# Attention: where ScalarE reads a side product, at the head of the next slot or between that slot's two exponentials

## The reference

```python
q, k, v = x @ Wq + bq, x @ Wk + bk, x @ Wv + bv      # 16 heads of 8
attn = q @ k.T / sqrt(8) + alibi                      # 1024 x 1024 for each head
attn = where(causal, attn, min); p = softmax(attn)
out = (p @ v) @ Wo + bo
x = layernorm(x + out); logits = x @ router_w.T + router_bias
```

## Time and profile before

| what | value |
|---|---|
| median of three runs | 1295.51 us |
| the profiled execution | 1296.66 us, of which the span is 1294.9 us |
| granted clock of TensorE, mean over the span | 0.87 |
| busy over the span | PE 972.5 us (75%), DVE 795.9 us (61%), ACT 549.7 us (42%), POOL 489.5 us (38%) |
| attention of layer 1, its slots | from about 349 to 957 us |
| ScalarE's exponentials (L2143) | 384, 299.1 us in all |
| VectorE's maxima (L2205) | 640, 374.6 us in all |

### The profile page before, as it was taken

How to read it: one execution, slowest core, us unless ns; L and a number is a source line. 1 busy time by engine, 2 the same in 40 slices (tenths; PEclk the granted TensorE clock), 3 DMA queues, 4 the chain that set the end, 5 groups by cost and what they waited for, 6 DMA issues and landing times. The chain is left out here.

```text
span 1294.9 us, 20993 instructions
## 1 busy us (share of the span) xinstructions
PE 972.5 (75%) x7024; PEld 549.3 (42%) x7024; DVE 795.9 (61%) x2147; ACT 549.7 (42%) x878; POOL 489.5 (38%) x484
## 2 busy tenths in 40 slices
PE   5772118962477799788987888788778989998892
PEld 4662016741222233232322333233237877885451
DVE  3757860022585789577884779778927542554664
ACT  1331004422134667566564666465564433431142
POOL 4001044525603700153002541043544544556775
PEclk8985558985569999898988999799999998999996
DMA  4224103421310301121010312225127755652122
GB/s 114 66 66 157 26 10 91 119 63 34 97 51 16 94 28 36 29 81 41 27 46 15 93 53 63 81 67 198 49 65 207 212 168 153 177 137 64 46 68 73
DMA packets 113439, 106.19 MB, mean 82 GB/s; under 512 B 17770, under 2 KB 95210, under 8 KB 112696
## 3 DMA queue, kind: packets, MB, share of 16 engines
q1 hardware_dynamic: 74216, 65.53, 16.8%
q0 software_dynamic: 12048, 25.71, 7.3%
q10 hardware_dynamic: 27072, 13.64, 3.7%
HBM read 59.60 MB, written 41.94 MB: 78 GB/s over the span
## 5 line engine op out<-in xcount | busy, mean ns | idle before, releaser
L2205 DVE TENSOR_REDUCE maxima<-psum 128x1 f32<-128x512 f32 (+3 forms) x640 | 374.6, 625 | 107.6 <-PE psum L2018 106.5
L2143 ACT ACTIVATE probs<-psum 128x1024 f32<-128x1024 f32 (+3 forms) x384 | 299.1, 809 | 266.6 <-PE psum L2038 264.4
L2018 PE MATMUL psum<-ka,qa 61*128 61x512 bf16 (+3 forms) x768 | 205.2, 358 | 30.8 <-ACT side_xT L1386 8.8
L2053 PE MATMUL psum<-probs,v_wide 128*32 128x512 f32 (+3 forms) x1536 | 178.0, 538 | 0.6 <-ACT outT L2115 0.4
L2038 PE MATMUL psum<-qa,ka 64*128 64x512 bf16 (+3 forms) x768 | 170.6, 341 | 1.5 <-ACT probs L2143 1.4
L1530 POOL DMA_INDIRECT sorted<-x_rows,to_row x76 | 76.3, 1003 | 209.2 <-ACT probs L2143 118.0
L2016 PE MATMUL psum<-mask 64*128 64x128 bf16 x512 | 98.1, 236 | 52.7 <-DVE maxima L2205 10.7
L2560 ACT ACTIVATE g_silu<-psum 128x512 f32<-128x512 f32 x80 | 47.8, 597 | 179.2 <-PE psum L2466 106.9
L1456 POOL DMA_INDIRECT w_gu<-expert_out,to_row x64 | 66.0, 1031 | 143.5 <-ACT probs L2143 100.9
L2018 PEld LDWEIGHTS psum<-ka,qa 61*128 61x128 bf16 x768 | 62.2, 98 | 113.2 <-DVE maxima L2205 67.5
L2016 PEld LDWEIGHTS psum<-mask 64*128 64x128 bf16 x512 | 42.2, 98 | 160.2 <-DVE maxima L2205 86.1
(11 more groups left out here) (326 smaller groups left out, 1614.4 us busy)
## 6 DMA issues: line engine op xcount, KB each, us to landing
g_rows<-sorted SPq DMA_DIRECT2D x192, 64.0 KB
expert_out<-g_y ACTq DMA_DIRECT2D x48, 256.0 KB, 2.7
w<-in_W SPq DMA_DIRECT2D x16, 256.0 KB, 3.0
w_gu<-in_gu SPq DMA_DIRECT2D x4, 1024.0 KB, 10.8
sorted<-blank SPq DMA_DIRECT2D x54, 64.0 KB
q_steps<-w_gu SPq DMA_DIRECT2D x12, 256.0 KB
k_steps<-w_gu SPq DMA_DIRECT2D x12, 256.0 KB
qa<-q_steps SPq DMA_DIRECT2D x30, 96.0 KB
```

Source lines behind the costliest of these rows:

```text
L2018: mm = pe.matmul(bank[:, h * width:(h + 1) * width], qa[b][at:at + ROWS_MAX, (h0 + h) % PER_SIDE, qt * P:(qt + 1) * P], ka[b][at:at + ROWS ...
L2053: mm = pe.matmul(B[OUT][32 * h:32 * (h + 1), q0 - c * HALF:HALF], v_wide[s.buf][:, j, h, PAD * (1 - c):PAD * (1 - c) + 32], probs[k % PRIN ...
L2143: act.activation(probs[k % PRING][:, 2 * pair:2 * pair + 2, 0:w], PS[:, 2 * pair:2 * pair + 2, 0:w], ACT.Exp).then_inc(exps, 1)
L2205: dve.tensor_reduce(maxima[:, seg, h0:h0 + heads, qt], bank[:, 0:heads * width].rearrange("p (h k) -> p h k", h=heads), AX.X, ALU.max).the ...
```

## The change

The call of `emit_side_scalar` leaves `beside(g)`, where it stood behind the first exponential of the slot, and is made at the head of the slot, ahead of the wait for the probability buffer and ahead of the first exponential. The rest of `beside` stays where it is. Nothing is added or removed; the order of instructions on the other engines is the same.

```diff
                 def beside(g):
                     b, r = divmod(g, BATCH_SLOTS)
-                    if g - 1 in SIDE_AT and SIDE_AT[g - 1][0] in ("turn_x", "q", "k", "turn_att", "turn_new"):
-                        emit_side_scalar(act, S, Q, SIDE_AT[g - 1])
                     if b + 1 < BATCH and SCALE_AT <= r < SCALE_AT + 4:
...
                         w = (c + 1) * HALF - q0
+                        g = s.n * SLOTS + k
+                        if g - 1 in SIDE_AT and SIDE_AT[g - 1][0] in ("turn_x", "q", "k", "turn_att", "turn_new"):
+                            emit_side_scalar(act, S, Q, SIDE_AT[g - 1])
                         if k >= PRING or not flags[0]:
                             act.wait_ge(pv, s.n * SLOTS + k - PRING + 1)
```

## The result

The changed kernel takes 1256.98 us (median of four runs, 1253.79 to 1259.1), the kernel before beside it 1291.38. The ratio is 0.972, with a 95% interval from 0.965 to 0.979. Timed a second time, six runs of it beside eleven of the kernel before, it took 1251.46 us against 1290.29: 0.968, from 0.963 to 0.972. The profiled execution of the changed kernel took 1253.79 us, its span 1252.1.

What follows compares the result with a forecast made beforehand. No engine is full; TensorE, the fullest, waits for side reads queued behind ScalarE exponentials. Stalls 32.8 us, less 1.5 for VectorE, plus 5 for the clock: 36 us off 1296.7 gives 1260, median 1259 us; range 1244 to 1280.

Steps and rivals of the forecast that it cites:

- The stalls: TensorE's 27 waits for ScalarE side reads in the attention stage, 44.3 us: moving the reads ahead saves 32.8 us.
- The q slot: Slot behind the q product: of TensorE's 1.76 us stall 1.46 goes, 0.30 stays; first exponential 0.14 later.
- the working of q: The q slot's 1.46 us gain, applied to each of fifteen slots with ScalarE idle before the exponential: 21.9 us.
- the queued slots: Seven slots with ScalarE running without pause: five give about 0.9 us each, 4.5 us; two with 768-column exponentials give 1.4.
- VectorE's deduction of 1.5 us: Three slots nearly filled by VectorE (4.20 busy in 5.00) can shrink only 0.8 us: 1.5 us off, 31.3 kept.
- The rows of maxima: Step edges: TensorE's one 7.1 us wait, at step 2, for transfers on SyncE's queue moves forward whole, costing the same.
- Rival 2: In the attention stage VectorE or a transfer takes half the gain, no clock gain: 1280 us; chance 15%.
- rival 3: Slots save, but rows of maxima or something behind the stage takes the gain: 1296 us, no change; chance 7%.
- The clock: TensorE's low clock stretches behind moved reads: 5 us saved, at most 18; six of eleven stand behind stalls only halved.
- rival 1: All eleven low clock stretches behind the attention stage's moved reads vanish: 1246 us; chance 13%.
- ScalarE as the pace-setter: Exponentials bound the slots, so each read put ahead costs its full length: 17 us slower, 1312 us; chance 3%.
- 0.62 + 0.13 + 0.10: Chances for faster by over 1%: the forecast, rival 1 and two thirds of rival 2, given as 0.86.

## Why the prediction was right

The mechanism was right and the time was met, 1259 against 1257. The terms, in the order of the prediction:

- **The stalls.** Forecast 32.8 us, measured 36.9. The q slot was forecast to keep 0.30 us of its stall and kept 0.24, and its first exponential, forecast 0.14 us later against its scores, came no later. The term was too small because I used the working of q, whose read is 0.68 us long, for the turned halves too, whose read is 0.59: those keep nothing. Two of the queued slots also kept less than the 0.9 us.
- **VectorE's deduction of 1.5 us** was hardly needed. It is 465.3 us busy in 575, and TensorE's waits for its maxima (L2016 and L2018) came to 15.4 us where they had been 14.8. These two rows together also stand above the 12.8 us of the negated maxima, which the prediction calls the next item.
- **The rows of maxima.** This is the step of the prediction that failed. It says that the wait of step 2 "moves forward whole and costs the same", and puts nothing in the sum for the other steps. For step 2 it held, 7.1 and 7.4 us. But I had looked only at the wait that was there, and not at how much room the same transfers had in steps 5, 9 and 13, which hold moved reads. Three waits of 2.4 to 3.1 us came up, 8.3 us together. Rival 2 and rival 3 both had this in them; it took a fifth of the gain, not half or all. That the stores and the clearings cause it is shown by the kernels that turn the queue's order round.
- **The clock.** Forecast 5 us, and what is left of the stage's 38.5 us is 9.9. The prediction let six of the eleven low stretches behind the reads stay, since their stalls are only halved. All eleven went, as in its rival 1, but three new ones, 24 us together, stand at the waits for the rows of maxima. So the term came out between the 5 us of the forecast and the 18 of the rival. The rule of the Trainium skill that activity releases the throttled state ("TensorE: Matmul & The Clock Gate", Part 1: The HAM clock gate) was weighed against one slot whose stall left the clock at 1.00; that was the weaker evidence. With the stalls filled the low stretches behind the reads went from eleven to none and the clock rose from 0.93 to 0.96, so with this rule, taken over many stalls, the traces agree.
- **ScalarE as the pace-setter**, the rival on the slower side, had nothing in it: even 0.87 us of scaling ahead of the first exponential made the kernel no slower.

The stalls and VectorE were 5.6 us better than the forecast, the clock 4.9, and the rows of maxima 8.3 worse; so they nearly cancelled. The sum was closer than its terms, and that part is luck. In the chances, 0.62 + 0.13 + 0.10 is 0.85 and not 0.86.

## What to carry to other kernels

In an engine's queue, put work in the order in which its inputs come, and look at who waits for its output: here a 0.6 us copy stood behind an exponential whose input came later, and the fullest engine waited for it. When stalls go, go through every transfer that ends a step and ask for its room, not only for the waits it has now; a transfer that just made it costs its shortfall and the low clock behind it. Idle time of TensorE cost more than its length here, by the low clock behind it.

## What the runs showed of the hardware

Eight matmuls whose results nobody uses, put into each stall, made the kernel 0.6% faster (0.991 to 0.998), by a granted clock of 0.96 in place of 0.93. One us at the low clock cost 0.3 to 0.4 us in this stage. In the kernel before, 11 of 27 stalls of 1.2 to 2.0 us had a low stretch in or behind them, in its second trace 12; with the stalls filled, none. The time ahead of the attention stage varied from 332 to 344 us over the traces with the same program there.
